# A due step for each group of products, in place of a table of places between the chunks

## What is computed

```python
u = jnp.einsum('bsd,hd->bsh', x, W_in) + b_in            # x: layer norm of the input
def step(state, u_t):
    s = jnp.tanh(u_t + state * gamma + beta)             # 1024 steps, one after the other
    return (s, s)
y = jnp.einsum('bsh,dh->bsd', states, W_out) + b_out
x = x + _layernorm(y)
...
gate = jax.nn.silu(_quantized_matmul(x, gate_w, gate_scale))     # x: layer norm of the x above
up = _quantized_matmul(x, up_w, up_scale)
return _quantized_matmul(gate * up, down_w, down_scale)          # 512 -> 1536 -> 512
```

## Time and profile before

| what | us |
|---|---|
| median of 3 runs | 581.17 (580.85 to 581.82) |
| the profiled execution | 580.79 |
| its span, first to last instruction | 579.0 |
| PE busy | 553.5 |
| DVE busy | 447.2 |
| ACT busy | 371.6 |
| POOL busy | 204.5 |

### The profile page before, as it was taken

How to read it: one execution, slowest core, us unless ns; L and a number is a source line. 1 busy time by engine, 2 the same in 40 slices (tenths; PEclk the granted TensorE clock), 3 DMA queues, 4 the chain that set the end, 5 groups by cost and what they waited for, 6 DMA issues and landing times.

```text
span 579.0 us, 11854 instructions
## 1 busy us (share of the span) xinstructions
PE 553.5 (96%) x2984; PEld 462.6 (80%) x2984; DVE 447.2 (77%) x2607; ACT 371.6 (64%) x2284; POOL 204.5 (35%) x339
## 2 busy tenths in 40 slices
PE   8999899899988999999999999999999999999993
PEld 5767667889776988788988799778986897889992
DVE  3689899996796888888988887789868988754313
ACT  3687687855686767866777677767776776523330
POOL 1214316435252323533334333152214341732622
PEclk9999999999998999999999999999999999999997
DMA  7878369800102001010102010020000200200000
GB/s 253 285 225 244 60 201 208 170 0 2 38 1 74 1 2 38 31 45 1 38 2 73 2 38 1 1 74 2 2 1 2 73 2 2 72 1 2 1 36 37
DMA packets 20069, 33.89 MB, mean 59 GB/s; under 512 B 2720, under 2 KB 4896, under 8 KB 20000
## 3 DMA queue, kind: packets, MB, share of 16 engines
q1 hardware_dynamic: 16544, 26.84, 13.8%
q0 software_dynamic: 3456, 6.29, 6.1%
HBM read 22.63 MB, written 4.19 MB: 46 GB/s over the span
## 4 chain that ended last, share of the span: by engine, by line
DVE 50%; ACT 24%; PE 17%; issue 5%; POOL 2%; SPq 0%; DMA 0%; POOLq 0%; DVEq 0%; ACTq 0%
DVE recur L1160 14%; ACT pairs L1466 10%; PE gate_up L1067 8%; DVE recur L1169 6%; DVE recur_second L1160 6%; DVE fused L1297 5%; ACT pairs L1450 4%; PE wide L1090 4%; ACT fused_hi L1509 3%; DVE peaks L1362 3%; ACT gated L1493 3%; PE wide L1026 3%; DVE powers L1345 2%; ACT pairs L1470 2%; DVE rounders L1352 2%
## 5 line engine op out<-in xcount | busy, mean ns | idle before, releaser
L1466 ACT ACTIVATE pairs<-recur 128x8 f32<-128x8 f32 x768 | 138.4, 180 | 100.2 <-DVE recur L1160 99.6
L1160 DVE TENSOR_TENSOR_SCAN recur<-recur,pairs 128x16 f32<-128x16 f32 x768 | 151.3, 197 | 56.0 <-ACT pairs L1466 51.8
L1592 POOL TENSOR_TENSOR fused_lo<-fused,fused_hi 128x256 fp32r<-128x256 f32 x96 | 71.1, 741 | 200.2 <-ACT fused_hi L1509 200.2
L1466 ACT ACTIVATE pairs<-recur_second 128x8 f32<-128x8 f32 x768 | 138.3, 180 | 0.0
L1160 DVE TENSOR_TENSOR_SCAN recur_second<-recur_second,pairs 128x16 f32<-128x16 f32 x768 | 133.4, 174 | 0.0
L1026 PE MATMUL wide<-w_out_sb,pairs 128*128 128x512 f32 x256 | 117.3, 608 | 5.7 <-ACT pairs L1466 5.7
L1067 PE MATMUL gate_up<-x_hi,gate_q 128*128 128x256 f32 x384 | 103.3, 302 | 3.5 <-DVE fused L1297 2.4
L1026 PEld LDWEIGHTS wide<-w_out_sb,pairs 128*128 128x128 f32 x256 | 74.4, 298 | 38.5 <-ACT pairs L1466 7.5
L1004 PE MATMUL wide<-x_norm_t,w_in_sb 128*128 128x256 f32 x448 | 101.0, 380 | 2.3 <-DVE y L1208 2.2
L1004 PEld LDWEIGHTS wide<-x_norm_t,w_in_sb 128*128 128x128 f32 x448 | 84.5, 190 | 16.0 <-issue 3.1
L1067 PE MATMUL gate_up<-x_lo,up_q 128*128 128x256 f32 x384 | 95.9, 283 | 0.0
(11 more groups left out here) (126 smaller groups left out, 763.8 us busy)
## 6 DMA issues: line engine op xcount, KB each, us to landing
x_in<-x SPq DMA_DIRECT2D x16, 256.0 KB, 3.3
x_res<-x SPq DMA_DIRECT2D x16, 256.0 KB, 3.2
out<-z SPq DMA_DIRECT2D x14, 256.0 KB, 2.5
w_in_sb<-w_in_t SPq DMA_DIRECT2D x4, 512.0 KB, 6.1
...
```

The source lines that it names most:

```text
L1160: eng.tensor_tensor_scan(preact_of[b].rearrange("p c k -> p (c k)"), factors_of[b].rearrange("p c k -> p (c k)"), pairs[:, (t - 1) % RING, ...
L1466: eng.activation(pairs[:, t % RING, columns, 0], preact_of[b][:, :, 1], ACT.Tanh).then_inc(s_state_of[b], 1)
L1592: eng.tensor_tensor(fused_lo[:, f, :], fused[:, f, :], fused_hi[:, f, :].bitcast(F32), ALU.subtract).then_inc(s_fused_lo, 1)
```

## The change

The table `BETWEEN`, `lay_first`, `lay_between` and the single chain are gone. Groups are declared kind by kind. A group is chained only to the one before it of its own kind (the key is the name's first word), and its rank is a due step from five small lists; `lay()` takes the group with the least due step among those that can begin. Three kinds of waits that the program always had are told to the planner: those for PSUM banks (u behind `y_copy`, u behind `first_u_copy`, y behind `u_copy` or `x1_low`), those of D(p,0), and those that keep T(p) behind G(p-1,11) and X(n) behind u(n-1,3). For PE's waits on other jobs a step is added (`TENSOR_MARGIN`). The ranks of the copies of T change a little. No instruction is added to an engine and none is taken away, and the waits written into the program are the same.

```diff
-    def tensor(self, name, steps, after, rank=0.0):
-        after = list(after)
-        if self.tensor_before is not None:
-            after.append((self.tensor_before, 0.0))
-        self.tensor_before = name
-        self.add("tensor", name, steps, after, rank)
...
-BETWEEN = {
-    1: {2: "y023", 9: "y1", 11: "x0 x1", 13: "u0", 14: "u1", 15: "u2 t0 u3 t1 Y001"},
...
+CHUNKS_FROM = [237, 352, 468, 637, 704, 878, 1000, 945]
+CHUNKS_PER_BLOCK = [8, 9.5, 8.5, 9, 11, 13, 3, 4.5]
...
+TENSOR_MARGIN = 1.0
...
+    def tensor(name, steps, after, due):
+
+        after = [(v, lag + (TENSOR_MARGIN if isinstance(v, tuple) else 0.0)) for v, lag in after]
+        if name[0] in before_on_tensor:
+            after.append((before_on_tensor[name[0]], 0.0))
+        before_on_tensor[name[0]] = name
+        t.add("tensor", name, steps, after, due)
...
     def project_u(n, m, k):
...
+            elif n >= 2:
+                after += [(v, 0.2) for v in rows("y", "y_copy", n - 2, m)]
...
+            if n == 1 and m == 2:
+                after += [(v, 0.2) for v in rows("y", "y_copy", 0, 0)]
+            tensor(("u", n, m), U_STEPS, after, INPUTS_FROM[n] + 7.0 * m)
...
+            tensor(("y", n, b, part), Y_STEPS / 4, after, ROWS_FROM[batch * n + b] + 0.1 * part)
...
-        t.tensor(("gate_up", p, i), GATE_UP_STEPS, after, k)
+        tensor(("gate_up", p, i), GATE_UP_STEPS, after, CHUNKS_FROM[p] + CHUNKS_PER_BLOCK[p] * i)
...
+        tensor(("down", p, i), DOWN_STEPS, after, CHUNKS_FROM[p] + CHUNKS_PER_BLOCK[p] * (i + LAG) - 4.0)
```

More of the change, by code:

```diff
@@ L248, in project_u, with project_y @@
                 after += [(("u_copy", n, m - 2, q), 0.2) for q in range(4)]
-            t.tensor(("u", n, m), U_STEPS, after, k)
+            elif n >= 2:
+                after += [(v, 0.2) for v in rows("y", "y_copy", n - 2, m)]
+            if n == 1 and m < 2:
+                after += [(("first_u_copy", m, jj), 0.2) for jj in range(4)]
+            if n == 1 and m == 2:
+                after += [(v, 0.2) for v in rows("y", "y_copy", 0, 0)]
+            tensor(("u", n, m), U_STEPS, after, INPUTS_FROM[n] + 7.0 * m)
             for q in range(4):
                 side("scalar", ("u_copy", n, m, q), [(("u", n, m), BEHIND_TENSOR)], k)
[L253 to L258, removed]
+    def project_y(n, b, k):
+        for part in range(4):
+            after = [(T * n + TH * (b + 1), 0.5)]
+            if part == 0:
+                if (n, b) == (0, 0):
+                    after += w_out_landed + rows_landed + [(("u_copy", 1, 0, q), 0.2) for q in range(4)]
+                elif n < LAST:
+                    after += [(("u_copy", n + 1, 2 + b, q), 0.2) for q in range(4)]
+                else:
+                    after += [(v, 0.2) for v in rows("low", "x1_low", n - 1, b)]
+            tensor(("y", n, b, part), Y_STEPS / 4, after, ROWS_FROM[batch * n + b] + 0.1 * part)
         for h in range(row_parts("y", n, b, LAST)):
@@ L281, in transpose_x1 @@
     def transpose_x1(n, b, after, k):
-        t.tensor(("t2", n, b), TRANSPOSE_STEPS, [(v, 0.2) for v in rows("r", "r_norm", n, b)] + after, k)
+        tensor(("t2", n, b), TRANSPOSE_STEPS, [(v, 0.2) for v in rows("r", "r_norm", n, b)] + after, ROWS_TURNED[batch * n + b])
         for h in range(2):
@@ L299, in down @@
     def down(p, i, k, after=()):
-        t.tensor(("down", p, i), DOWN_STEPS, [(("low", p, i), 0.1), *after], k)
+        after = [(("low", p, i), 0.1), *after]
+        if i == 0 and p < LAST - 1:
+            after += [(v, 0.2) for b in range(batch) for v in rows("low", "x1_low", p, b)]
+        elif i == 0:
+            after += [(v, 0.2) for b in range(batch) for v in rows("z", "z_copy", p - 1, b)]
+        tensor(("down", p, i), DOWN_STEPS, after, CHUNKS_FROM[p] + CHUNKS_PER_BLOCK[p] * (i + LAG) - 4.0)
     def norm_z(n, b, after, k, k_copy=None):
@@ L431, in split_next @@
                 scaled = [(v, 0.1) for v in rows("y", "y_copy", p, b)]
[L432 to L439 removed]
+            if p > 0:
+                scaled += [(("gate_up", p - 1, KI - 1), 0.0)]
@@ L440, in lay_first @@
+            transpose_x1(p, b, scaled, rank(p, 4) if p > 0 else FIRST_X1_RANK)
         for i in range(KI):
-            after = list(low) if i == 0 else []
-            if i % 4 == 0:
+            after = [(v, 0.2) for b in range(batch) for v in rows("low", "x1_low", p, b)] if i == 0 else []
+            if p == 0 and i % 4 == 0:
                 after += converted(range(2 * i, 2 * i + 8))
-            if i == 2:
+            if p == 0 and i == 2:
                 after += converted(i for i in range(NP) if not by_transfer(i))
-            if i == FIRST_Y_AT_CHUNK:
-                project_y(p + 1, 0, rank(n - 1, 6))
@@ L500, in timetable @@
-    for i in range(KI):
-        low = [(v, 0.2) for b in range(batch) for v in rows("low", "x1_low", LAST, b)] if i == 0 else []
-        gate_up(LAST, i, low, rank(LAST, 4.5) + 0.01 * i)
-        if i >= LAG:
-            down(LAST, i - LAG, rank(NB, 7) + 0.1 * i)
-    for i in range(KI - LAG, KI):
-        down(LAST, i, rank(NB, 9))
-    for b in range(batch):
-        norm_z(LAST, b, ("down", LAST, KI - 1), rank(NB, 10 + b))
+            gate_up(p, i, after, rank(p + 1, 4.5) + 0.01 * i)
+            down(p, i, rank(p + 1, 7) + 0.1 * i, after=converted([GATE_UP_PIECES + i]) if p == 0 else ())
```

102 lines of the change are left out of this document (26 added, 76 removed), and 5 rows, old and new, of the table BETWEEN.

## The result

The changed kernel takes 574.94 us (574.87 to 575.73, 4 runs), the kernel before 581.01 (580.35 to 581.82) beside it: ratio 0.989, 95% interval 0.986 to 0.992, some 6.1 us faster. The profiled execution has a span of 573.1 us, before 579.0. The forecast was 574.5, in a range of 572 to 579; of the span it was 572.3.

The account below looks back on a forecast made before the run. The end was taken as a state's moment plus PE's work behind the y taking it. Gains of 5.2 (behind y(4,1)) and 2.4 (recurrence) less 0.9 make 6.7 us: 581.17 - 6.7 = 574.5, range 572.0 to 579.0.

Parts of the forecast that it names:

- The moment of a state plus PE's work behind it: What sets the end: when a state is there, plus PE's work behind the y taking it; before, y(7,1): 501.77 + 67.1 + 10.2.
- The walk along PE's order: PE's new order timed group by group from y(0,1) at 82.21; y(2,0) at 177.3, so its 3.87 us wait goes.
- the sum hangs on state 640: At y(4,1), which waits for state 640 at 324.57: the sum starts there, so an earlier state brings the end earlier too.
- The term of 2.4: Recurrence: without its two long stops every later state, and the end, comes 1.0 + 1.4 = 2.4 us earlier; bounds 0 and 2.4.
- Behind y(4,1): From y(4,1)'s start on: 238.9 us against 244.3, a gain of 5.4, less 0.2 for the restart: 5.2 us.
- The allowance of 0.9: Set against the gain for new short ACT stops and longer ways to `fused_lo` or `x_lo`: 0.9 us, ends 0 and 3.
- The stops at steps 93 and 334: Recurrence, at u(1,2)'s copy and G(1,0)'s silu: ACT stands 1.07 and 1.18 us; both causes were to go.
- other stops take their place: Recurrence: the lower bound of its gain, 0 instead of 2.4 us, if new stops replace the two long ones.
- The clock falls in block 0: Rival: after the new wait at G(0,0), a lower clock stops the recurrence 0 to 1.4 us; price 1.0, 575.5; chance 0.20.
- The clock behind the 2.16 us: At 61.05, u(1,2)'s wait for y(0,0)'s copy: 2.16 us idle, said not to be followed by the lower clock.
- D's shorter lead: Rival: D behind G(i+2) waits 0.3 us in some 55 chunks of blocks 1 to 5, 16 us slower, 590; chance 0.06.
- The recurrence eats it: Rival: 768 two-chain steps each take 8 ns more, states come 6 us later, no change, 580.5 to 581.5; chance 0.08.

## Why the prediction was right, and which step was not

**The time.** 574.94 against 574.5, with a range that holds it; of the span, 573.1 against 572.3.

**The frame.** "The moment of a state plus PE's work behind it" was right: the largest wait alone was worth 1.5 us of its 5.4, and with the late y moved too 5.2. But the state from which the changed kernel's end hangs is 128, at y(0,1), and not 640.

**The walk along PE's order** in the head held within 0.4 us: T(0,1) at 104.6 for 105.0, G(0,0) at 108.72 for 108.5, y(1,1) at 149.86 for 149.5, y(2,0) at 177.65 for 177.3. y(2,0) has no wait and the full clock. That it is so close is in part luck: y(0,1), where the walk begins, started 1.54 us earlier than the 82.21 it took, and 1.0 us of unforeseen wait at u(2,2) and 0.6 more for `x_lo` made up for that.

**The step that failed: "the sum hangs on state 640".** The walk found waits of 1.9, 0.3 and 0.8 us at y(2,1), y(3,1) and y(4,1), but against the old states. Then the states were moved forward by 2.4 us, and the end with them. With earlier states those waits can't stand: PE comes to y(4,1) with its own backlog, 0.93 us behind state 640. The recurrence's part should have been cut to what PE could use. Measured, state 640 came 2.1 us earlier (322.35 for 324.48), y(4,1) only 1.3 (323.28 for 324.57). The term of 2.4 was worth 1.3. The last tanh ahead of state 640, in the kernel before and in the changed one:

```profile
324.29 0.19 ACT L1466 ACTIVATE pairs<-recur_second 128x8 f32<-128x8 f32 x1
...
322.17 0.18 ACT L1415 ACTIVATE pairs<-recur_second 128x8 f32<-128x8 f32 x1
```

**Behind y(4,1)** the forecast was 5.2 us less; it was 579.0 - 324.57 = 254.4 less 573.1 - 323.28 = 249.8, 4.6. D(5,11) waited 0.41, with 0.20 at T(6,1) ahead of it, for the 1.7 given, G(7,0) under 0.1 for 0.4, and D(7,11) 0.47 for 0.85. G(7,4)'s 0.76 was not foreseen: I had looked at POOL's `fused_lo` as a lag behind G, and not at what else stands in POOL's order there. 1.3 + 4.6 is 5.9; the forecast was 5.2 + 2.4 - 0.9 = 6.7. The allowance of 0.9 for what the rows don't show pointed the right way and took half of the miss; it was not worked out from rows, so that the time came out within 0.5 us is to that extent luck.

**The recurrence.** The stops at steps 93 and 334 went, as forecast. A new one of 1.07 us came at step 156. Against the kernel before the states were 1.55 us earlier at 128, 0.2 at 192, not earlier at 320, 1.65 at 384 and 2.1 at 640; smaller stops behind that took 0.85, so that the last state is at 500.36 for 501.64, 1.3 us earlier. That "other stops take their place" was the lower bound given; half of it happened.

**The rivals.** *The clock falls in block 0*: it did, which I had at 0.20, and it cost PE 1.6 us at G(0,0) and G(0,1). It did not cost the end that much: with the wait filled, at full clock, y(1,0) waited for its state, and 0.2 us were left. The Trainium skill (TensorE: Matmul & The Clock Gate, section "HAM oscillation — how this bites in real kernels") says that PE which a long enough wait leaves idle begins its next work cold, at half rate. The trace agrees for 3.53 us. At u(1,2) the clock fell behind 2.15 and 2.17 us in two profiles and did not behind 2.16 and 2.17 in two others. The clock behind the 2.16 us, on which the prediction leaned, is not in its but in the stretch shown above. *D's shorter lead*: no D waited in the middle of a block. *The recurrence eats it*: steps took no longer; only single stops moved. The chances as listed add up to 0.86, 0.08 and 0.06 for faster, same and slower, where the prediction ends on 0.85, 0.08 and 0.07.

**What is open.** Whether DVE or POOL is held at step 156 goes with the place of T(0,0) in six profiles; why was not tested. The part of a low clock behind u(1,2) in the time of the kernel before is inferred from mean clocks, not seen in place. How the changed kernel's 4.4 us behind y(0,1) divide among its moves was not run on that kernel; the two moves of y that were tried on the kernel before can give as much.
